# First layer's edge loop of a four-layer graph network: three shared PSUM banks, and operands of VectorE read from PSUM

## The reference, cut to what matters

```python
xl = (x @ W_l + b_l).reshape(n, HEADS, C)          # HEADS, C = 4, 16
xr = (x @ W_r + b_r).reshape(n, HEADS, C)
e = (edge_attr @ W_e).reshape(-1, HEADS, C)        # 16 attributes per edge
g = leaky_relu(xl[src] + xr[dst] + e, 0.2)
logits = einsum('ehc,hc->eh', g, att)
ex = exp(logits - segment_max(logits, dst)[dst])
alpha = ex / (segment_sum(ex, dst)[dst] + 1e-16)
out = segment_sum(xl[src] * alpha[..., None], dst) + bias
out = gelu(batch_norm(out) * gamma + beta + x)
```

## Time and profile before

| | us |
|---|---|
| median of three runs | 8234.38 |
| span of the profiled execution, first to last instruction | 6576.8 |
| the edge loop of layer 0: first gather's start to last gather's start | 429.6 to 2839.9 |
| TensorE's mean granted clock over the span | 0.735 |

### The profile page before, as it was taken

One profiled execution on the slowest core, in us unless ns is written; L12 is line 12 of the kernel. 1 busy time (PEld: TensorE's weight loads), 2 busy tenths in 40 slices (PEclk: granted clock), 3 DMA queues, 4 the chain that ended last, 5 costly groups with the idle time before them and its releaser, 6 DMA issues. The chain is left out here.

```text
span 6576.8 us, 115590 instructions
## 1 busy us (share of the span) xinstructions
PE 5007.3 (76%) x35178; PEld 4266.4 (65%) x35178; DVE 3022.6 (46%) x3931; ACT 1799.8 (27%) x3844; POOL 3882.2 (59%) x3427
## 2 busy tenths in 40 slices
PE   2338888888888888841999957877878787771898
PEld 2315665665566655531999957777777777771898
DVE  7757777777777777746322131111111111113322
ACT  0024555555555545510000012222222222220000
POOL 5748788888788888750000047777777777773000
PEclk9668888888888888955999955555555555555898
DMA  9335555555555555522999846666666666652895
GB/s 358 77 84 141 151 153 152 143 150 150 154 155 146 150 149 154 153 61 84 329 366 366 312 128 202 204 203 203 205 204 203 206 204 197 202 178 62 336 389 215
DMA packets 659138, 1262.13 MB, mean 192 GB/s; under 512 B 167881, under 2 KB 467466, under 8 KB 633268
## 3 DMA queue, kind: packets, MB, share of 16 engines
q1 hardware_dynamic: 381076, 726.95, 32.8%
q10 hardware_dynamic: 168480, 416.21, 18.9%
q0 software_dynamic: 109184, 115.05, 9.8%
HBM read 924.66 MB, written 490.51 MB: 215 GB/s over the span
## 5 line engine op out<-in xcount | busy, mean ns | idle before, releaser
L696 POOL DMA_INDIRECT att_gl<-tab_l,att_ix x1568 | 1933.5, 1233 | 487.6 <-issue 472.3
L1184 POOL DMA_INDIRECT sum_gl<-tab_l,sum_ixs x1568 | 1572.3, 1003 | 524.7 <-issue 477.8
L937 ACT ACTIVATE att_acc<-att_pc 128x392 bf16<-128x392 f32 x2352 | 1083.3, 497 | 1324.1 <-PE att_pc L715 1122.6
L712 PE MATMUL att_pc<-att_ohl,att_ohv 128*128 128x392 bf16 x2352 | 863.0, 367 | 272.0 <-DVE att_ohl L812 271.7
L1134 PE MATMUL sum_pm<-sum_msg,sum_S 128*128 128x64 f32 x3136 | 680.0, 407 | 425.6 <-ACT sum_msg L1158 425.5
L1134 PEld LDWEIGHTS sum_pm<-sum_msg,sum_S 128*128 128x128 f32 x3136 | 647.0, 314 | 465.7 <-issue 264.7
L715 PE MATMUL att_pc<-att_acc,att_ohv 128*128 128x392 bf16 x2352 | 855.7, 364 | 116.3 <-ACT att_acc L937 112.7
L1104 DVE TENSOR_TENSOR sum_t<-sum_pb,sum_gl 128x512 f32<-128x512 f32 x196 | 135.6, 692 | 1692.1 <-DMA sum_gl<-tab_l,sum_ixs 1692.1
L1116 PE MATMUL sum_pb<-sum_wbs,sum_ea 64*128 64x64 f32 x3136 | 694.5, 419 | 27.4 <-DMA sum_ea<-in_ea64T 27.4
L731 PEld LDWEIGHTS att_pl<-att_xe,att_S 128*128 128x128 f32 x3136 | 599.3, 216 | 159.8 <-issue 137.3
L1116 PEld LDWEIGHTS sum_pb<-sum_wbs,sum_ea 64*128 64x128 f32 x3136 | 676.1, 329 | 39.0 <-DMA sum_ea<-in_ea64T 27.6
(11 more groups left out here) (360 smaller groups left out, 5190.2 us busy)
## 6 DMA issues: line engine op xcount, KB each, us to landing
A<-att_acc SPq DMA_DIRECT2D x2352, 98.0 KB
l_a<-A SPq DMA_DIRECT2D x147, 1568.0 KB, 9.2
l_at<-AT SPq DMA_DIRECT2D x98, 1568.0 KB
att_dall<-in_dst ACTq DMA_DIRECT2D x224, 448.0 KB
sum_dall<-in_dst SPq DMA_DIRECT2D x196, 512.0 KB, 4.8
sum_a<-A SPq DMA_DIRECT2D x49, 1568.0 KB, 10.1
AT<-sum_at ACTq DMA_DIRECT2D x49, 1568.0 KB, 5.4
tot<-att_o ACTq DMA_DIRECT2D x56, 1022.0 KB
```

Source lines behind the costliest of these rows:

```text
L696: nc.gpsimd.indirect_dma_start(out=gl[s][:, c, :], out_offset=None, in_=g.tab_l, in_offset=bass.IndirectOffsetOnAxis(ap=ix[s][:, c:c + 1], ...
L712: nc.tensor.matmul(pc[c][m % 2][:, 0:LO], ohv[c][h][:, m, :, 0], ohl[c][h][:, m // 2, :, m % 2], start=True, stop=False)
L937: nc.scalar.activation(acc[c][n % CR][:, :], pc[c][m % 2][:, 0:LO], ACT.Copy).then_inc(s_acc[c], 1)
L1184: nc.gpsimd.indirect_dma_start(out=gl[q][:, j, :], out_offset=None, in_=g.tab_l, in_offset=bass.IndirectOffsetOnAxis(ap=ixs[q][:, j:j + 1] ...
```

## The change

Four PSUM banks of items become three, used in rotation by both chains together: item n of chain c takes bank (2n + c) mod 3. The wait before an item's first matmul now names the other chain's copies, since the item three places earlier used the bank. The fourth bank becomes `pd`. It holds the attention row `attp`, copied there once, and the destination columns `dstp` of two batches, copied once for each batch at k = 0, with a semaphore between copy and use. L800 and L825 read these in place of `dst` and `att`. L849 reads the exponentials where TensorE has put them, in `pt`, in place of ScalarE's copy in `xb`; its wait for that copy stays. `scores` gets a wait for the messages before TensorE writes to `pt` again.

```diff
+    PCB = 3
-        pc = [[st.ps(f"pc{c}_{b}", [P, 512]) for b in range(2)] for c in range(CH)]
+        pc = [st.ps(f"pc{b}", [P, 512]) for b in range(PCB)]
+        pd = st.ps("pd", [P, 512])
+        exbp = pt[:, P:P + GH].rearrange("p (h c) -> p c h", h=HEADS)
+        attp, dstp = pd[:, 0:D], pd[:, D:D + R * GB]
...
-                    if not known(n, 2):
-                        pe.wait_ge(s_acc[c], n + (-1))
-                    nc.tensor.matmul(pc[c][m % 2][:, 0:LO], ohv[c][h][:, m, :, 0], ohl[c][h][:, m // 2, :, m % 2],
+                    bank = pc[(2 * (at0[t] + m) + c) % PCB]
+                    if not known(n, 2 - c):
+                        pe.wait_ge(s_acc[1 - c], n + (-1 if c == 0 else 0))
+                    nc.tensor.matmul(bank[:, 0:LO], ohv[c][h][:, m, :, 0], ohl[c][h][:, m // 2, :, m % 2],
...
                 def scores(b, s):
                     wait_reuse(pe, s_xb, b)
+                    wait_reuse(pe, s_msg, b * NQ)
...
+                    if k == 0:
+                        v.tensor_copy(dstp[:, s * GB:(s + 1) * GB], dst[:, bass.ds(i * (R * GB) + t * GQ, GB)])\
+                            .then_inc(s_pd, 1)
+                        dve.wait_ge(s_pd, i * R + (s + 2))
                     v.tensor_tensor(S[s][:, k * GQ:(k + 1) * GQ, :], dall[k][:, :, :],
-                                    spread(dst[:, bass.ds(i * (R * GB) + t * GQ, GQ)].unsqueeze(2), [P, GQ, P]),
+                                    spread(dstp[:, t * GQ:(t + 1) * GQ].unsqueeze(2), [P, GQ, P]),
...
-                    step(v.tensor_tensor(t2[:, :, :], t2[:, :, :], spread(att[:, :].unsqueeze(1), [P, GQ, D]),
+                    step(v.tensor_tensor(t2[:, :, :], t2[:, :, :], spread(attp.unsqueeze(1), [P, GQ, D]),
...
-                            spread(exb[:, k * GQ:(k + 1) * GQ, :].unsqueeze(3), [P, GQ, HEADS, C]), ALU.mult)\
+                            spread(exbp[:, k * GQ:(k + 1) * GQ, :].unsqueeze(3), [P, GQ, HEADS, C]), ALU.mult)\
...
+                v.tensor_copy(attp, att[:, :]).then_inc(s_pd, 1)
```

More of the change, by code:

```diff
@@ L655, in edge_loop @@
             "S", "pl", "t1", "L", "LT", "sub", "exp", "back", "xb", "exm", "msg", "sum", "ev", "top"))
-        s_ends = st.sem("ends")
+        s_ends, s_pd = st.sem("ends"), st.sem("pd")
         s_out = [st.sem(f"out{s}") for s in range(R)]
@@ L709, in item @@
                         pe.wait_ge(s_oh[c], i * (2 * SL) + (2 * t + 2))
-                    if not known(n, 2):
-                        pe.wait_ge(s_acc[c], n + (-1))
-                    nc.tensor.matmul(pc[c][m % 2][:, 0:LO], ohv[c][h][:, m, :, 0], ohl[c][h][:, m // 2, :, m % 2],
+                    bank = pc[(2 * (at0[t] + m) + c) % PCB]
+                    if not known(n, 2 - c):
+                        pe.wait_ge(s_acc[1 - c], n + (-1 if c == 0 else 0))
+                    nc.tensor.matmul(bank[:, 0:LO], ohv[c][h][:, m, :, 0], ohl[c][h][:, m // 2, :, m % 2],
                                      start=True, stop=False)
                     wait_reuse(pe, s_acc[c], n)
-                    nc.tensor.matmul(pc[c][m % 2][:, 0:LO], ohv[c][h][:, m, :, 1], acc[c][(at0[t] + m - 1) % CR][:, :],
+                    nc.tensor.matmul(bank[:, 0:LO], ohv[c][h][:, m, :, 1], acc[c][(at0[t] + m - 1) % CR][:, :],
                                      start=False, stop=True).then_inc(s_mm[c], 1)
@@ L936, in count @@
                     act.wait_ge(s_mm[c], i * (CB * CJ) + (n + 1))
-                    nc.scalar.activation(acc[c][n % CR][:, :], pc[c][m % 2][:, 0:LO], ACT.Copy).then_inc(s_acc[c], 1)
+                    nc.scalar.activation(acc[c][n % CR][:, :], pc[(2 * n + c) % PCB][:, 0:LO], ACT.Copy).then_inc(s_acc[c], 1)
                 def turn(i):
```

## The result

The changed kernel is slower: 8451.85 us median (8446.94 to 8488.45), ratio 1.0234 (95% interval 1.0172 to 1.0296) to the kernel before. The prediction, 8140, had the wrong sign. In medians this comparison gives 207 us, beside 8245.03 of the kernel before, which had been timed a fourth time by then. Two later comparisons, each beside the kernel before on one chip, gave 1.0193 (1.0152 to 1.0233) and 1.0184 (1.0123 to 1.0245), 177 and 157 us in medians. I take these two: the change costs about 1.9%. The ratios leave out runs at a lower granted clock, of which there were two (8338.31 us of the kernel before, 8867.06 us of the same with a gap behind each gather), while the medians keep them.

A forecast was written before the change was run, and what follows sets the result against it. POOL's 1568 gathers in sequence were taken to bound the loop. A 100 us gain less 5 us for copies gave -95 us, carried from 8234.4 to 8139, rounded to 8140; range 8060 to 8248, the forecast's own 8090 to 8175.

The forecast's parts named there:

- The carried difference: Outside the profiled span: the other 1657.6 us of the median stay, so the span's 95 us gain carries one to one.
- POOL is never held up by another engine: Edge loop: POOL's busy and issue time fill 2405 of 2415 us, so 1568 gathers in sequence set its length.
- the 100 us that were to reach the end: Edge loop: of 148 us saved on POOL, 100 arrive, between 148 by POOL's chain and 69 by TensorE's.
- The read port: Gathers beside VectorE: instructions with two SBUF operands stretch them; relieving L800, L825 and L849 saves POOL 148 us.
- my rivals: Alternatives to the forecast: larger gain 0.10, other engines just beneath POOL 0.16, lock not by operand 0.08, slow PSUM reads 0.05.
- The small terms: VectorE and TensorE: column copies add 5 us, PSUM reads leave durations unchanged, three banks add 0 us.
- The copies: VectorE, columns into PSUM: 56 small copies and one larger, 0.24 us each, 13.5 us in all, 5 on the path.
- rival E: VectorE's three changed lines: PSUM operands read more slowly, making VectorE the bound; 8320 us with 50% more, chance 0.05.
- Three banks cost nothing: TensorE's item matmuls at L717: waits on the other chain's copies are already met, no new stall, 0 us.

The follow-up runs named there:

- later profile: Kernel before, unedited, profiled anew on the same chip as the changed kernel: 8279.08 us, ratio 0.9996.
- five pairs: Kernel before against changed kernel, each pair alike: unedited, SP's program shortened, gathers paced by group, long gap, short gap; unedited pair 8279.08 and 8442.05 us.
- SP's program short: Both kernels with SP reading no row numbers and storing one item in three at fixed places: before 7874.4 us, changed 8289.57 us.

## Why the prediction was wrong, point by point

**The carried difference failed first.** "No row shows what the other 1657.6 us of the median hold; the loop is in the span, so I carry the change one to one." The profiles of the same kernel taken later have spans of 8402.0 and 8251.2 us beside times of 8403.83 and 8253.01. What stood between span and median was not beside the execution; it was an edge loop of 3619 us in place of 2415 and slower stages behind it. A median 25% above the span was the sign that the trace showed another execution, and it deserved a rival of its own and a wide range.

**"POOL is never held up by another engine" failed with it.** In the ordinary loop POOL waits 1327 us for messages, so the loop is not as long as 1568 gathers one after the other, and the 100 us that were to reach the end became a loss of 157 to 177. POOL gathers in a burst of 28, and while the burst lasts the other engines all but stand. The end of such a burst, kernel before, in its later profile:

```profile
1064.31 0.51 PE L715 MATMUL att_pc<-att_acc,att_ohv 128*128 128x392 bf16 x1 [0.37 <-issue]
...
1067.82 1.50 PE L753 MATMUL att_pm<-att_msg,att_S 128*128 128x69 f32 x6
...
1086.56 0.94 POOL L696 DMA_INDIRECT att_gl<-tab_l,att_ix  x1 [0.30 <-issue]
1091.82 0.50 ACT L937 ACTIVATE att_acc<-att_pc 128x392 bf16<-128x392 f32 x1 [24.68 <-remote]
...
1092.17 1.09 DVE L800 TENSOR_TENSOR att_S<-att_dall,att_dst 128x896 f32<-128x896 int32 x1 [28.64 <-remote]
```

The copy needs the item of 1064.31 and the compare needs the sums of 1067.82. Both come 22 us or more after these matmuls had started and, by their modelled ends, finished, and 4 us after the last gather's end. The waits of the later profile of before, to be read against the earlier trace rows:

```profile
POOL att_gl L696 <- DVE att_msg L849: 1327.4, 49, 37.9
ACT att_acc L937 <- remote: 1135.4, 238, 27.5
DVE att_S L800 <- remote: 1030.9, 50, 30.8
```

A "remote" wait has no instruction of the trace that ended it just then. The semaphore that ends these waits is TensorE's in every case: that of the items for L937, that of the sums for L800. It isn't the stores' landing, which I had taken ScalarE to wait for: in 120 of its waits, 911 us, the instruction that waits for the store had run already, 6 us before the copy in the median. Over both engines the "remote" waits in the loop are 2816 us for the kernel before and 2895 for the changed one. There are none in the first trace, none without gathers and none in the four runs with gaps. So in a burst two things come late, SP's instructions and TensorE's signals. What delays them is not shown.

**The read port was right in mechanism, and in size at most.** Gathers are stretched by VectorE's instructions with two SBUF operands. In the later profile of before, 75 of the 89 gathers that start under L800 take over 1 us, 17 of 36 under L825 and 3 of 23 under L849. In the changed kernel beside it none of 117 under L810, L835 and L859 does, as I had said. Relieving the three lines took 72, 56, 92, 44 and 32 ns from the mean gather in five pairs, 50 to 144 us of POOL's time where I had forecast 148. That agrees with the Trainium skill, "SBUF — State Buffer", "Who interferes with whom", on operands, and not with its inference for `tensor_tensor` and descriptors.

**What the relief does downstream is where the sign came from.** The prediction asked who waits for POOL and not what a denser train of gathers does to others. My reading is that VectorE's stretching of gathers loosened the train, and that this feeds on itself: where items get through, VectorE works, gathers stretch, and more items get through. The change takes that away. The order in time fits. Counted in the later profile of before, from the ninth gather of a burst on, SP's and ScalarE's queues start 15 packets a us over the three gathers ahead of one of 1.6 us or more, 28 during it and 51 over the three behind it (69 such gathers); around gathers under 0.97 us it is 29, 28 and 20. That is a count and no experiment: no run lengthened gathers by VectorE alone, and the step from denser gathers to fewer items is argued, not shown. What the runs do show is that the loss stands only where gathers follow each other without a gap. With a gap put in by hand the same change is 54 and 40 us faster; without one 157 to 177 us slower, and 415 us with SP's program short. None of my rivals named this. The Trainium skill, "DMA: Bandwidth & Descriptors", "SWDGE vs HWDGE vs iDMA", calls transfers issued from SP or ScalarE immune to VectorE's lock on descriptor generation. No run here contradicts that, but SP's issuing is far from independent of the gathers themselves, by the steps of 0.70 us.

**The small terms held.** The copies are 56 in 10.7 us, 191 ns each. The compares, products and messages, changed kernel beside the earlier trace rows, have not grown:

```profile
L810 DVE TENSOR_TENSOR att_S<-att_dall,att_pd 128x896 f32<-128x896 int32 x224 | 243.5, 1087 | 30.4 <-DVE att_L L837 22.6 <-issue 3.6
L835 DVE TENSOR_TENSOR att_t<-att_t,att_pd 128x448 f32<-128x448 f32 x224 | 139.0, 620 | 7.7
...
L859 DVE TENSOR_TENSOR att_msg<-att_gl,att_pt 128x448 f32<-128x448 f32 x224 | 123.9, 616 | 117.2 <-ACT att_xb L930 117.2
```

So rival E, slower through slow PSUM reads, is not what happened. Three banks cost nothing: 1.0014 alone, and L717 does not wait for ScalarE.

**Open.** Why the first execution was free of this. What in the chip ties SP's instructions and TensorE's signals to POOL's gathers. Whether the change costs anything on the slower chips. Why chips differ (the kernel before from 8240 to 8416 us); the 747 against 607 items copied in bursts on the chips where the kernel before takes 8285 and 8396 us fit the feedback, but no run tests it.

## What to carry to other kernels

Compare a profile's span with the median before reading anything else: where they differ by more than a per cent, its bound is not the bound of the runs, and the first thing to get is another profile. Where one engine issues many small indirect transfers in bursts, ask what the others get done while a burst lasts; here spreading the same gathers over the items was worth 9%, and making them faster cost 2%. A change that is right for the engine it helps has to be tried together with what it now lets run unchecked.

## What the runs showed of the hardware that was not expected

- While GpSimd issues gathers back to back (one each 1.25 us), SP's sequencer takes 0.70 us, or a multiple, for single register instructions of 37 ns: about 1600 us of a loop of 3619. Without gathers it is about 40 us, with a gap of about 1.3 us between them about 105 us. It doesn't always happen: the first execution has gathers 1.25 us apart too and about 50 us of such steps.
- In such a burst ScalarE and VectorE wait on TensorE's semaphores until it is over, 28.64 us in the rows above, though TensorE's matmuls had started and by their modelled ends finished over 20 us before: 2816 us in sum over both engines in the loop, and none with gaps of 0.9 to 1.3 us between the gathers.
- The queues of SP and ScalarE move little then, 169 packets in 20 us against 1829 in the first execution, because little is issued to them.
- A gather that starts under a VectorE instruction with two SBUF operands ends 0.82 us after it (in the median), and takes its usual 0.94 us where one operand is in PSUM.
- Two profiles of one program can have spans of 6576.8 and 8402.0 us, and the kernel before can differ by 2% between chips (8240 to 8416 us).
